# Latent attention with its scores computed twice: keys along the partitions instead of turned probabilities

## The reference

```python
x = x + _L0_xcond_ref(_layernorm(x), cond, ctx, ...)      # 16 batches: self attention, cross attention, GELU block
x = x + _L0_ffn_ref(_layernorm(x), ...)                   # mixture of 64 experts, top 8, and a shared one
x = x + _L1_xcond_ref(ctx, _layernorm(x), cond, cond, ...)  # latent attention, 16 batches
x = x + _L1_ffn_ref(_layernorm(x), ...)                   # mixture of 8 experts, top 1
```

```python
x = layer_norm(x, ln1_w, ln1_b)                           # here x is the context
lat = layer_norm(latents, ln2_w, ln2_b)
lat = lat * (1.0 + scale[:, None, :]) + shift[:, None, :]
q = jnp.einsum('bld,ed->ble', lat, Wq)
kv_in = jnp.concatenate((x, lat), axis=-2)                # 375 + 112 = 487 keys
kv = jnp.einsum('bld,ed->ble', kv_in, Wkv)
k, v = jnp.split(kv, 2, axis=-1)                          # 16 heads of 64
logits = jnp.einsum('bhqd,bhkd->bhqk', q * attn_scale, k * attn_scale)
w = jax.nn.softmax(logits.astype(jnp.float32), axis=-1)
out = jnp.einsum('bhqk,bhkd->bhqd', w, v)
return jnp.einsum('ble,de->bld', out, Wo)
```

## Time and profile before

| | |
|---|---|
| median of three runs | 2726.28 us (2725.03 to 2726.6) |
| the profiled execution | 2729.83 us |
| its span | 2727.8 us |
| PE busy | 2649.5 us (97%) |
| DVE, ACT, POOL busy | 56%, 40%, 31% |
| mean granted clock | 0.989 |

### The profile page before, as it was taken

How to read it: one execution, slowest core, us unless ns; L and a number is a source line. 1 busy time by engine, 2 the same in 40 slices (tenths; PEclk the granted TensorE clock), 3 DMA queues, 4 the chain that set the end, 5 groups by cost and what they waited for, 6 DMA issues and landing times.

```text
span 2727.8 us, 60629 instructions
## 1 busy us (share of the span) xinstructions
PE 2649.5 (97%) x18079; PEld 1836.0 (67%) x18080; DVE 1517.2 (56%) x4423; ACT 1104.7 (40%) x2903; POOL 857.3 (31%) x1548
## 2 busy tenths in 40 slices
PE   9999999999999999998899989999999999999698
PEld 6777777777777777776566655656656656666597
DVE  5555565555555656555666655565566565554332
ACT  2444434433443444333466634333334433334232
POOL 2122121222221212222555434434433434420353
PEclk9999999999999999999999999999999999999799
...
GB/s 247 4 9 7 9 9 9 9 9 5 7 7 8 9 9 9 9 4 113 199 255 256 184 60 36 23 23 33 31 26 22 22 22 29 35 72 5 103 181 25
DMA packets 87779, 145.65 MB, mean 53 GB/s; under 512 B 22418, under 2 KB 64399, under 8 KB 86176
## 3 DMA queue, kind: packets, MB, share of 16 engines
...
...
## 4 chain that ended last, share of the span: by engine, by line
PE 87%; ACT 5%; DVE 3%; issue 3%; POOL 1%; DMA 1%; DVEq 0%; ACTq 0%; POOLq 0%; SPq 0%
PE psG L1060 16%; PE psG L1054 14%; PE psG L1048 11%; PE psG L1072 8%; PE psG L1495 5%; PE psO L1014 5%; ACT probs L1752 4%; PE psG L989 4%; PE psG L1001 3%; PE psG L1561 3%; PE psO L1572 3%; PE psO L1507 2%; PE psO L1048 2%; PE psT L1001 2%; PE psT L989 2%
## 5 line engine op out<-in xcount | busy, mean ns | idle before, releaser
L1060 PE MATMUL psG<-W,ctxT 128*125 128x512 f32 (+2 forms) x896 | 405.1, 595 | 0.0
L1054 PE MATMUL psG<-ctxT,W 128*128 128x375 f32 (+1 forms) x1024 | 387.3, 526 | 2.4 <-ACT ctxT L2002 1.3
L1054 PEld LDWEIGHTS psG<-ctxT,W 128*128 128x128 f32 x1024 | 189.7, 190 | 162.1 <-issue 107.6
L1752 ACT ACTIVATE probs<-psG,nmax 112x375 f32<-112x375 f32 (+1 forms) x384 | 233.5, 619 | 151.2 <-DVE nmax L2202 151.2
L1060 PEld LDWEIGHTS psG<-W,ctxT 128*125 128x125 f32 (+2 forms) x896 | 160.4, 186 | 175.4 <-issue 170.8
L2202 DVE TENSOR_REDUCE nmax<-psG 112x1 f32<-112x375 f32 (+1 forms) x384 | 208.6, 599 | 71.2 <-PE psG L989 65.3
L1048 PEld LDWEIGHTS psG<-hT,W 128*128 128x128 f32 x2064 | 236.6, 192 | 16.5 <-ACT hT L1783 14.3
L1048 PE MATMUL psG<-hT,W 128*128 128x112 f32 x2064 | 241.8, 275 | 0.9 <-ACT hT L1783 0.9
L1014 PEld LDWEIGHTS psO<-probsT,v 125*64 125x64 f32 (+2 forms) x3584 | 173.3, 136 | 65.4 <-issue 60.7
...
L1014 PE MATMUL psO<-probsT,v 125*64 125x112 f32 (+2 forms) x3584 | 200.5, 262 | 0.0
L775 POOL DMA_INDIRECT W<-normed_rows,ids x144 | 136.5, 948 | 126.1 <-PE psG L1477 99.0
...
## 6 DMA issues: line engine op xcount, KB each, us to landing
...
ctxT<-in_ctxT SPq DMA_DIRECT2D x16, 375.0 KB, 3.1
kT<-in_ctx SPq DMA_DIRECT2D x16, 375.0 KB
normed_rows<-hrow SPq DMA_DIRECT2D x32, 112.0 KB, 1.9
...
```

Of the source, the lines that this page charges most:

```text
L1054: mm = nc.tensor.matmul(bank[:, 0:n], wt[:, c, n0 + j * P:n0 + (j + 1) * P], src[:, c, 0:n], start=(c == 0), stop=(c == DC - 1))
L1060: mm = nc.tensor.matmul(bank[0:kn, 0:512], src[:, c, k0:k0 + kn], wt[:, c, n0 + half * 512:n0 + (half + 1) * 512], start=(c == 0), stop=(c ...
L1752: nc.scalar.activation(probs[:, 2 * (u % 2) + i, 0:keys], pair_bank(order, scores_slot(u), i)[0:T, 0:keys], ACT.Exp, bias=nmax[:, h:h + 1] ...
```

## The change

Each pair's scores are now computed twice in the latent stage.

The first time (`row_scores`, `row_maxima`, `row_sums`) they stand as before, queries along the partitions, and serve for the maxima and the sums alone. They move out of the attention into `rest_L` of the batch before, between the halves of the values, and use `psO` and `psT` in turn. The exponentials that ACT computes there are thrown away; only their sums stay.

The second time (`scores` in `latent_attention`) the keys are the stationary operand, in chunks of 122, so that the tile has keys along the partitions, and no transpose follows. A maximum belongs to a query, which is now a column, so it can't be a bias per partition. ACT stores the maxima of eight heads in DRAM (`store_maxima`, 112x8) and loads them back to 122 partitions, 896 numbers in each (`spread_maxima`), twice per batch, for heads 0 to 7 and 8 to 15. DVE adds them to both heads' scores at once (122x896, from PSUM and SBUF to SBUF), ACT exponentiates 122x896 from SBUF to SBUF, and PE multiplies with the values.

Both copies of the turned tiles and all turns are gone from this stage. The queries are made before `project_out`, and all four `valuesL` after it. The first block's attention is unchanged, but the weights' semaphores are now shared by two loads each, and its users wait for both. `kT2` is one column wider.

The diff, cut:

```diff
-w_in = {n: sem("w_in_" + n) for n in ("nw", "q1", "k1", "v1", "o1", "k2", "v2", "q2", "o2", "f1", "f2")}
+maxima_out, maxima_in, probsT_taken = sem("maxima_out"), sem("maxima_in"), sem("probsT_taken")
+w_in = {n: sem("w_in_" + n) for n in ("nw", "q1", "k1")}
+for pair in (("v1", "k2"), ("v2", "o1"), ("q2", "o2"), ("f1", "f2")):
+  w_in[pair[0]] = w_in[pair[1]] = sem("w_in_" + "_".join(pair))
...
+maxB = W[0:KC, 17408:17408 + H * T].rearrange("p (g t h) -> p g h t", g=2, t=T)
+lessmax = W[0:KC, 17408 + H * T:17408 + H * T + 4 * NK * T].rearrange("p (w i n) -> p w i n", w=2, i=2)
+maxd = nc.dram_tensor("maxima", (2, T, H // 2), F32, kind="Internal").ap()
+def pair_banks(slot):
+  return psT[:, 0:2, :] if slot == 2 else psG[:, 2 * slot:2 * slot + 2, :]
+def maxima_bank(u, i):
+  return (psO, psT)[u % 2][0:T, i, 0:KV]
...
-      pe.wait_ge(w_in["v1"], 16)
+      pe.wait_ge(w_in["v1"], 32)
...
-  def rest_L(r=None):
-    valuesL(1)
-    queriesL()
+  def half_values(c, half):
+    k0, kn = chunks(KV, KC)[c]
+    bank = bank_for_dve() if half else bank_for_act()
+    values(wkvL, INNER, ctxT, k0, kn, half, bank).then_inc(dve_full if half else act_full, 1)
+  def row_scores(u):
+    u0 = unit.now()
+    if u >= 2:
+      pe.wait_ge(probs_ready, u0 + 2 * u - 2)
+    for i in range(2):
+      nc.tensor.matmul(maxima_bank(u, i), qT2[DH * i:DH * i + DH, u, :], kT2[DH * i:DH * i + DH, u, 0:KV],
+              start=True, stop=True).then_inc(scores_ready, 1)
+  def rest_L(r, keys_a, keys_d):
+    pe.wait_ge(act_evac, keys_a)
+    pe.wait_ge(dve_evac, keys_d)
+    row_scores(0)
     if r is not None:
       tile_logits1(r)
-    valuesL(2)
-    valuesL(3)
+    valuesL(0)
     if r is not None:
       tile_ranks1(r)
+      pe.wait_ge(S0.ranks_read, B + r + 1)
+    row_scores(1)
+    row_scores(2)
+    for u in range(3, PAIRS):
+      half_values((u - 1) // 2, (u - 1) % 2)
+      row_scores(u)
+    half_values(NK - 1, 1)
+  def latent_attention(banks, late=None):
+    ch = chunks(KV, KC)
+    u0, a0, d0 = unit.now(), ca.now(), cd.now()
+    free_for_outputs = {}
+    def scores(u):
+      if u == 2:
+        pe.wait_ge(probs_ready, u0 + H)
+      if u > 2:
+        pe.wait_ge(copied_dve, d0 + u - 2)
+      for i in range(2):
+        if u < 2 and LATENT[u][i] in banks:
+          pe.wait_ge(*banks[LATENT[u][i]])
+      for c, (k0, kn) in enumerate(ch):
+        for i in range(2):
+          mm = nc.tensor.matmul(pair_banks(u % 3)[0:KC, i, c * T:(c + 1) * T],
+                     kT2[DH * i:DH * i + DH, u, k0:k0 + KC], qT2[DH * i:DH * i + DH, u, :],
+                     start=True, stop=True)
+          if c == len(ch) - 1:
+            mm.then_inc(probsT_ready, 1)
+    def outputs(u):
+      pe.wait_ge(copied_act, a0 + u + 1)
+      if u in free_for_outputs:
+        pe.wait_ge(*free_for_outputs[u])
+      for c, (k0, kn) in enumerate(ch):
+        for i in range(2):
+          h = 2 * u + i
+          mm = nc.tensor.matmul(psO[DH * i:DH * i + DH, u // 4, (u % 4) * T:(u % 4 + 1) * T],
+                     v2[0:kn, c, h * DH:(h + 1) * DH],
+                     probsT[0:kn, u % 2, i, c * T:(c + 1) * T],
+                     start=(c == 0), stop=(c == len(ch) - 1))
+      if u % 4 == 3:
+        mm.then_inc(outputs_ready, 1)
+      elif u < 6:
+        mm.then_inc(probsT_taken, 1)
+    for k in range(0, PAIRS, 2):
+      scores(k)
+      scores(k + 1)
+      if k == 0 and late:
+        pe.wait_ge(probs_ready, u0 + H)
+        free_for_outputs = late()
+      if k:
+        outputs(k - 2)
+        outputs(k - 1)
+    outputs(PAIRS - 2)
+    outputs(PAIRS - 1)
+    for g in range(2):
+      spread_half(spreadL, g, psT[:, g, :])
+    unit.next(H)
+    ca.next(PAIRS)
...
   project_T(wkvL, ctxT[:, :, S:KV], 512, 4, bank_for_dve()).then_inc(dve_full, 1)
+  pe.wait_ge(act_evac, act.now())
+  pe.wait_ge(dve_evac, dve.now())
+  row_scores(0)
+  row_scores(1)
   valuesL(NK - 1)
+  for u in range(2, PAIRS):
+    row_scores(u)
+  assert ca.now() == cd.now() == COPIES_BEFORE
   def batchL(b, more, more2, routed=True):
-    if more:
-      banks = held(2, 2)
-    else:
-      banks = held(0, 0)
-    if routed:
-      banks["T"] = (S0.ranks_read, B + b - 1)
-    attention(LATENT, qT2, kT2, v2, KV, KC, spreadL, banks, None,
-         (lambda: late_kv(b + 1)) if more and routed else None)
+    latent_attention(held(2, 2), (lambda: late_kv(b + 1)) if more and routed else None)
     dve.skip()
     if not routed:
       transpose_kv(1)
       evacuated()
     if more:
       keysL()
-      valuesL(0)
+      queriesL()
+      keys_a, keys_d = act.now(), dve.now()
     project_out(woL, oT, IC)
     if routed:
       tile_T1(b - 1)
     if more:
-      rest_L(b - 1 if routed else None)
+      rest_L(b - 1 if routed else None, keys_a, keys_d)
     else:
...
-  def values_queriesL():
+  cd, taken = Tally(), Tally()
+  cd.next(COPIES_BEFORE)
+  def row_sums(u):
+    u0 = unit.now()
+    for i in range(2):
+      act.wait_ge(max_ready, u0 + 2 * u + i + 1)
+      h = 2 * u + i
+      nc.scalar.activation(probs[:, 2 * (u % 2) + i, 0:KV], maxima_bank(u, i), ACT.Exp, bias=nmax[:, h:h + 1],
+                accum_out=rsum[:, h:h + 1]).then_inc(probs_ready, 1)
+  def store_maxima(b, g):
+    act.wait_ge(max_ready, unit.now() + 8 * g + 8)
+    act.dma_start(maxd[g], nmax[:, 8 * g:8 * g + 8]).then_inc(maxima_out, 16)
+  def spread_maxima(b, g):
+    act.wait_ge(maxima_out, 32 * b + 16 * g + 16)
+    act.dma_start(W[0:KC, 17408 + 8 * T * g:17408 + 8 * T * (g + 1)],
+           maxd[g].rearrange("t h -> (t h)").partition_broadcast(KC)).then_inc(maxima_in, 16)
+  def rest_L(b):
+    row_sums(0)
     valuesL(0)
+    row_sums(1)
+    row_sums(2)
     valuesL(1)
-    copy4(qT2[:, 0:4, :], QSCALE)
+    row_sums(3)
+    store_maxima(b, 0)
+    row_sums(4)
     valuesL(2)
+    row_sums(5)
+    spread_maxima(b, 0)
+    row_sums(6)
     valuesL(3)
+    row_sums(7)
+    store_maxima(b, 1)
+  def latent_attention(b, late=None):
+    d0 = cd.now()
+    for u in range(PAIRS):
+      act.wait_ge(copied_dve, d0 + u + 1)
+      if u in (2, 3, 4):
+        act.wait_ge(probsT_taken, taken.next())
+      if u == 5:
+        act.wait_ge(outputs_ready, made.now() + 1)
+      if u in (6, 7):
+        act.wait_ge(probsT_taken, taken.next())
+      nc.scalar.activation(probsT[0:KC, u % 2].rearrange("p i n -> p (i n)"),
+                lessmax[:, u % 2].rearrange("p i n -> p (i n)"), ACT.Exp).then_inc(copied_act, 1)
+      if u == 0:
+        spread_maxima(b, 1)
+      if late and u in (1, 3):
+        late(u // 2 + 2)
+    unit.next(H)
+    cd.next(PAIRS)
+    made.next(2)
+    for g in range(2):
...
   batchL(0, True, True, True)
   with act.Fori(1, B - 2) as b:
     jobs.enter(b - 1, ACTL_JOBS)
     unit.enter(b - 1, 16)
     scaled.enter(b - 1, 2)
+    cd.enter(b - 1, 8)
+    taken.enter(b - 1, 5)
+    made.enter(b - 1, 2)
...
-  def rest_L(r=None):
-    valuesL(1)
-    copy4(qT2[:, 4:8, :], QSCALE)
+  ca = Tally()
+  ca.next(COPIES_BEFORE)
+  def row_maxima(u):
+    u0 = unit.now()
+    for i in range(2):
+      dve.wait_ge(scores_ready, u0 + 2 * u + i + 1)
+      nc.vector.tensor_reduce(nmax[:, 2 * u + i:2 * u + i + 1], maxima_bank(u, i), AXX, ALU.max,
+                  negate=True).then_inc(max_ready, 1)
+  def rest_L(r, behind):
+    row_maxima(0)
     if r is not None:
       choose1(r)
-    valuesL(2)
-    valuesL(3)
+    valuesL(0)
+    if r is not None:
+      places1(r)
+      slots1(r, 0)
+      slots1(r, 1)
+    if behind:
+      behind(4)
+    for u in range(1, PAIRS):
+      row_maxima(u)
+      if u in (3, 5, 7):
+        valuesL(u // 2)
+  def latent_attention(b, between=None, late=None):
+    u0, a0 = unit.now(), ca.now()
+    for k in range(0, PAIRS, 2):
+      if k == 4:
+        invert_half(spreadL, 0, u0 + H // 2)
+      if between:
+        between(k // 2, 0)
+      for u in (k, k + 1):
+        dve.wait_ge(probsT_ready, u0 + 2 * u + 2)
+        if u == 0 or u == 4:
+          dve.wait_ge(maxima_in, 32 * b + 4 * u + 16)
+        if u > 1:
+          dve.wait_ge(copied_act, a0 + u - 1)
+        h = 2 * u % 8
+        nc.vector.tensor_tensor(
+          lessmax[:, u % 2].rearrange("p i (c t) -> p i c t", c=NK),
+          pair_banks(u % 3)[0:KC, :, 0:NK * T].rearrange("p i (c t) -> p i c t", c=NK),
+          maxB[:, u // 4, h:h + 2, :].unsqueeze(2).broadcast_to([KC, 2, NK, T]),
+          ALU.add).then_inc(copied_dve, 1)
+      if k == 0 and late:
+        late()
+      if between:
+        between(k // 2, 1)
+    unit.next(H)
+    ca.next(PAIRS)
+    invert_half(spreadL, 1, unit.now())
+    scaled_outputs()
...
     settled()
     nc.vector.bn_aggr(mv[0:T, 1, :], st[0:T, 1, :]).then_inc(S0.measured, 1)
     if more:
-      rest_L(b - 1 if turned else None)
+      rest_L(b - 1 if turned else None, behind)
     else:
       choose1(b - 1)
-    if turned:
       places1(b - 1)
       slots1(b - 1, 0)
       slots1(b - 1, 1)
```

59 lines of the change are left out of this document (39 added, 20 removed).

## The result

The changed kernel takes 2953.18 us (2951.68 to 2955.51, 4 runs), the kernel before on the same chip 2725.66 us (2724.49 to 2726.6, 4 runs): a ratio of 1.0833, 95% interval 1.0821 to 1.0846. The forecast was 2947 us, and slower.

A forecast was written before the change was run, and what follows sets the result against it. PE was taken as the bound. A batch: 58.2 + 1.6 + 10.3 + 2.2 = 72.3 us against 58.63, so 205 us over fifteen intervals, plus 16 for the first batch: 2951, as median 2947 us (2862 to 3022).

The forecast's parts named there:

- PE's own work: Latent batch: turns at 0.84 us a pair give way to new scores at 0.93; 58.2 us a batch, no gain.
- What bounds the kernel: Whole kernel: PE is full, DVE and ACT are not; a change gains only what it takes off PE.
- New waits behind the projection: `tile_logits1` waits 0.4 us for `hTt`, `row_scores(1)` 0.7 for `places1`, `row_scores(3)` 0.5 for exponentials: 1.6 us a batch.
- The load on two engines: Spread maxima to 122 partitions get two DMA engines of sixteen: 11.0 us from issue to landing.
- The chain of the two loads: Latent attention: second load issued after the first lands; 30.1 us against 19.8, so PE idles 10.3 us a batch in two gaps.
- Rival 3: DVE's add reads maxima with a step of eight numbers, taking 2.1 us instead of 1.1; 3020 us, chance 0.10.
- The clock: PE runs at 1.2 GHz for a while behind the second load's gap: 2.2 us a batch (0 to 3.4).
- The first batch: Batch 0 has no cover for the loads: keys at about 1665.5 instead of 1649.63, 16 us.
- Rival 1: The loads of maxima land in 3 to 4.5 us and hide; 2753 us, chance 0.12.
- The range: Total time: 2862 to 3022 us; downwards clock 2.2, waits 1.6, quicker loads 2 a batch; upwards 19 GB/s, 75 us.

The follow-up runs named there:

- e5: The changed kernel with maxima loaded to 128 partitions instead of 122 and the add reading with unit step (other heads' maxima): 2815.41 us, ratio 1.0288.
- e7: e5 with row scores reordered in `rest_L`: pairs 3 and 4, and 5 and 6, side by side, two value halves between: 2807.06 us, ratio 1.0262.
- e3: The changed kernel, still 122 partitions, with DVE's add reading maxima at a step of one number instead of eight: 2929.75 us, ratio 1.0747.
- e2: The changed kernel with the spread maxima loaded to 128 partitions instead of 122, add's step unchanged: 2847.89 us, ratio 1.0449.

## Why the prediction was right, and where its terms were not

The direction, the mechanism and the sum held. That the sum came so near is luck: PE's work and its busy time at a slow clock were 2.4 and 1.5 us too small, its idle time 3.6 us too large, and the errors cancelled. A batch, forecast against the mean of fourteen:

| term | forecast | measured |
|---|---|---|
| PE's own work at full clock | 58.2 | 60.6 (e5) |
| what PE is busy beyond that, mostly the slow clock | 2.2 | 64.31 - 60.6 = 3.7 |
| PE idle: waits of `rest_L` and gaps of the loads | 1.6 + 10.3 | 8.28 |
| a batch | 72.3 | 72.59 |

- **What bounds the kernel.** Right: e5, with loads and step repaired, has PE 98% busy and is still slower than before, so there was nothing left to gain beside PE.
- **PE's own work, "no gain".** This is the term that failed most, 2.4 us a batch or 36 us in all. New scores take 0.94 to 0.98 us a pair from start to start, not 0.93: 0.2 us. The larger part is that the forecast took both prices, the row scores' 0.91 and 1.7 for half a chunk, from rows where each stood among its like, 2.6 us a step; alternating a step takes 2.92, and there are six: 1.8 us. e7 shows that it is the order that costs, by getting 1.14 us back. The remaining 0.4 us are small things in the timelines of the kernel before and of e5: the transpose of `tile_T1` 0.29 us instead of 0.19, `tile_logits1` 0.41 instead of 0.33, the rank products 0.47 instead of 0.40, and the last two outputs 1.76 instead of 1.69 each. The 0.70 us that the forecast calls a wait was not idle time (PE is busy for 58.08 of the 58.18 us), but it went with the turns all the same.
- **New waits behind the projection.** `tile_logits1` 0.25 (0.4 forecast), `row_scores(1)` 0.55 (0.7), `row_scores(3)` 0.23 (0.5): the right three, 1.03 us instead of 1.6.
- **The load on two engines.** Right, and shown by the four other row counts. Its price was right too: 11.0 us forecast, 11.1 and 10.3 in the mean. In flight it is a little quicker than forecast, since the engines carry 26 GB/s each, not the 24.4 of the five-engine row. The Trainium skill's rule on the largest divisor ("DMA: Bandwidth & Descriptors", section "Why a DMA increments its semaphore by 16 and not by 1") agrees with the shares of 122, 121, 125 and 127 rows, 0.13, 0.67, 0.32 and 0.06, and nothing speaks against it in the 0.86 of 128.
- **The chain of the two loads.** Right in order, too large in size. The forecast had 32.3 us from the first issue to the attention's end, slow clock included; in the batch shown it is 2166.94 - 2135.81 = 31.1. The larger error is in what PE would have had to do meanwhile, 19.8 us. The same piece of PE's stream, from the half of the values at 2134.34 to the end of the outputs, in the changed kernel and in e5:

```profile
2134.34:2166.94 32.60, 27.18 (x286) 19.59 (x284) 21.92 (x28) 13.19 (x23) 9.79 (x32) 0.90 0.13 45
1772.35:1795.90 23.55, 23.27 (x287) 16.75 (x285) 16.52 (x28) 13.09 (x23) 9.45 (x31) 1.00 0.21 64
```

The changed kernel takes 9.1 us more, against 10.3 + 2.2 = 12.5 forecast; with the 1.47 us ahead of the issue taken off, PE's own work and waits there are 22.1 us, so the loads had 2.3 us more cover than reckoned. In the mean batch loads and clock cost 72.59 - 60.6 - 1.03 = 11.0 us. Where two gaps of 4 to 5 us were expected, the batch shown has one of 1.88 and five of 0.58 to 0.90; over the stage PE is busy 89% of the time, not near 80%, and the adds that wait for a load wait 3.6 us each, not some 5.

- **Rival 3, the step.** Its mechanism is true at two thirds of its price: 1.77 us an add, not 2.1, against 1.08 (the forecast had 1.1). I gave it 0.10, and by mechanism the outcome is this rival's on top of the two engines, at the time of the forecast without it. In the changed kernel it moves little, since the loads come last (e3: 23 us); with the loads repaired it is worth more, 65.95 - 62.62 = 3.3 us a batch (e2 against e5).
- **The clock.** Right in kind, too small in size. PE is busy 3.7 us a batch longer than in e5's undisturbed batch; e2, at a clock of 1.00, has 61.33 us busy in the mean, so some 0.7 of the 3.7 come with a stream broken up by waits, and 3.0 are the clock's, against 2.2. It comes back whole when the long gaps go: 1.00 in e2 and e5.
- **The first batch.** Keys of batch 1 were forecast at 1665.5 and stand at 1666.63, 17.0 us later than before.
- **Rival 1** (the loads hide, 2753 us) would not have come true even with 128 rows: 2847.89, since step and alternation were not in its sum.
- **The range.** Its three terms downwards, 2.2, 1.6 and 2, make 5.8 us a batch, not 5.7; nothing hangs on it.

Of the 13.96 us a batch, then: 6.6 go with two engines (e2), 3.3 with the step (e5), 0.4 with the order (e7 against e5), and 3.6 remain: the row scores' remaining alternations and waits, and 0.8 of loads that land late (62.21 in the mean, 61.38 undisturbed). The shares hold in this order of repairs; the step alone, mended first, gave 1.9 (e3).
